# Relative attention: the order of VectorE's PSUM copy and its row maxima within a unit

## The chip, the cores and the metric

The kernel runs on one core of one Trainium2 chip. The metric is the time of one execution on the device in microseconds (us), as the median of repeated runs.

## The reference

An audio tower of five stages over x of 32 sequences x 256 frames x 7 channels: a signature tokeniser (255 tokens of 128 features for each sequence), a fuzzy attention, a top-1 mixture of 8 experts, a relative-position attention, and a top-2 mixture of 64 experts with a shared expert. Each but the first works on a layer norm of h and adds to h. The change is in the fourth, which computes this:

```python
    b, t, c = x.shape            # 32, 255, 128 here
    h, hd = (H, HD)              # 8 heads of 16
    q = x @ Wq + bq
    k = x @ Wk + bk
    v = x @ Wv + bv
    ...
    idx = _rel_index(t)          # clip(key - query, -68, 68) + 68
    rk2 = rel_k[idx]
    rv2 = rel_v[idx]
    attn1 = jnp.einsum('bhqd,bhkd->bhqk', rq, rk)
    attn2 = jnp.einsum('bhqd,qkd->bhqk', rq, rk2)
    attn = jax.nn.softmax((attn1 + attn2) * (1.0 / math.sqrt(c)), axis=-1)
    w1 = jnp.einsum('bhqk,bhkd->bhqd', attn, rv)
    w2 = jnp.einsum('bhqk,qkd->bhqd', attn, rv2)
    out = (w1 + w2).transpose(0, 2, 1, 3).reshape(b, t, c)
    return out @ Wo + bo
```

## The kernel before

The kernel is one program of stages, one behind the other. `relative_attention` is the stage of the change. Each engine has its own instruction queue, written out by hand, and works it off in order; semaphores join them. The stage takes the 32 sequences `b` one by one, each in NU = 4 units `u`; a unit is four blocks of 128 rows, a row being one query of one head. So there are 128 units, and each engine runs its `slot(b, u, r)` 128 times, between a `head` and a `tail`. The work is pipelined over units: in slot (b, u)

- TensorE first turns the exponentials of unit (b, u): `turn_e`, eight 128x128 transposes (L1748) into the one PSUM tile `t_ps`, ended by the semaphore `t_done`. Then come small products of other sequences and the content scores of the unit two ahead (`content`, L1707, three matmuls for each block), `turn_o` (L1792; in u = 0 and u = 2, it waits for this unit's `eT_v`), `positions` (L1762, from the turned exponentials with the relative values, into `rv_ps`), in odd units `values` (L1781), and last `position_scores` of the unit two ahead (L1727), which end its scores and raise `s_done`.
- ScalarE copies its half of the turned exponentials (`read_eT`, L1975), takes the exponentials of the next unit (`exps`, L1966, four instructions, with the maxima as bias, raising `e_ready`), and then has, among others, `read_n` (L1994), in u = 2 `read_q` (L1947, L1949), in every second sequence `read_odds` (L2026, u = 0), and `read_rv` (L1982), which copies `rv_ps` out and raises `rv_read`.
- VectorE takes the row maxima of the next unit (`maxima`, L2299) and copies its half of the turned exponentials (`read_eT`, L2307), and then has the work listed by unit in its `slot`: for instance the low part of the keys (`keys_remainder`, L2251, u = 2), for which TensorE's `project_q` (L1691) waits, and the choice of experts (`route`).

`turn_e` starts with these waits, so both the exponentials and ScalarE's last copy out of `t_ps` stand before it (`rv_ps` lies in `t_ps`):

```python
pe.wait_ge(e_ready, NU * b + u + 1)
if after(b, 1) or u > 0:
    pe.wait_ge(rv_read, NU * b + u)
```

There are two score tiles (`s_ps[u % 2]`) and two of exponentials (`e[u % 2]`), but one `t_ps`. GpSimd scatters rows of the next stage and SyncE moves rows through HBM beside all this.

Of the kernel before, what the change touches and what calls it, by code (L numbers as in the profile page):

```python
# [1463 lines left out]
def relative_attention(nc, K, h, mean, rstd, stats, y0_rows, o_rows, q_rows, weights, x1_slots, xT_rows, placed, y0_out, sent):  # L1464
# [3 lines left out]
    with Bench(nc, "rel") as m:  # L1468
# [93 lines left out]
        def have(b):  # L1562
            return not isinstance(b, int) or 0 <= b < B

        def after(b, n):
            return not isinstance(b, int) or b >= n
# [17 lines left out]
        def ahead(b, u, n):  # L1584
            return (b + (u + n) // NU, (u + n) % NU)
# [29 lines left out]
        with nc.Block(no_gpsimd_drain=True) as block:  # L1615
# [586 lines left out]
            def _(dve):  # L2202
                def add_rows(c):
                    hc = h[:, c * CH:(c + 1) * CH, :]
                    dve.wait_ge(y_in[c], 16)
                    nc.vector.tensor_tensor(hc, hc, y_at[c], ALU.add).then_inc(rows_added, 1)
# [58 lines left out]
                def queries_remainder(b, r, pairs):  # L2265

                    dve.wait_ge(rest_ready, b + 1)
                    if b == 0:
                        dve.wait_ge(zeroed, 4)
                    if after(b, 2):  # L2270
                        dve.wait_ge(s_done, NU * (b - 1))
                    for k in pairs:
                        nc.vector.tensor_copy(of_heads(q_head[r][1], k), of_pair(1, k).bitcast(FP32)).then_inc(ql_ready, 1)  # L2273

                def position_queries(b, r):

                    dve.wait_ge(q_in, 16 * 2 * QUAD * (b + 1))
                    if after(b, 2):
                        dve.wait_ge(s_done, NU * (b - 1))
                    nc.vector.tensor_tensor(  # L2280
                        q_pos[r][:], q_rep[:].rearrange("p h (g i) -> p g h i", i=QUAD),
                        mask4[:].unsqueeze(1).unsqueeze(1).to_broadcast([P, T // (2 * QUAD), H, QUAD]),
                        ALU.mult).then_inc(qp_ready, 1)

                def read_v(b, r):

                    dve.wait_ge(v_done, b + 1)
                    if after(b, 2):
                        dve.wait_ge(pv_done, 2 * b - 2)
                    heads = "p s (h d) -> p s h d"  # L2290
                    for k, bias_sb in ((0, bv_sb[:].unsqueeze(1).to_broadcast([P, 2, D])), (1, vends_sb[:])):
                        last = nc.vector.tensor_tensor(
                            v[r][:, :, k, :, 0:HD], pa.rearrange("p (s h d) -> p s h d", s=2, h=H),
                            bias_sb.rearrange(heads, h=H), ALU.add)
                    last.then_inc(v_ready, 1)

                def maxima(b, u):
                    dve.wait_ge(s_done, NU * b + u + 1)
                    nc.vector.tensor_reduce(neg_max[u % 2][:], s_ps[u % 2][:, :, 0:L], AX.X, ALU.max, negate=True)\  # L2299
                        .then_inc(max_ready, 1)  # L2300

                def read_eT(b, u):
                    s, n = u // 2, UB * (u % 2)
                    dve.wait_ge(t_done, NU * b + u + 1)
                    if after(b, 1):
                        dve.wait_ge(pv_done, 2 * b + s - 1)
                    nc.vector.tensor_copy(eT[s][:, 1, n:n + UB], t_ps[:, 1]).then_inc(eT_v, 1)  # L2307

                def read_ot(b, s):
                    j = 2 * b + s  # L2310
                    dve.wait_ge(ot_done, j + 1)
                    nc.vector.tensor_copy(o_tok[:], o_of[:, :, 0:HD + 1]).then_inc(ot_read, 1)

                def combine(b, s):

                    j = 2 * b + s
                    dve.wait_ge(ot_read, j + 1)
                    dve.wait_ge(rv_in, 16 * (j + 1))
                    nc.vector.reciprocal(rden[:], o_tok[:, :, HD:HD + 1].rearrange("p k c -> p (k c)"))\
                        .then_inc(rden_ready, 1)  # L2320
                    nc.vector.tensor_tensor(o_sum[:], o_tok[:, :, 0:HD],
                                            rv_tok[:, s, :].rearrange("p (h d) -> p h d", d=HD), ALU.add)\
                        .then_inc(sum_ready, 1)
                    dve.wait_ge(rden_ready, j + 1)
                    dve.wait_ge(sum_ready, j + 1)
                    if s == 1 or after(b, 1):
                        dve.wait_ge(oT_done, j)
                    nc.vector.tensor_tensor(o_norm[:], o_sum[:], rden[:].unsqueeze(2).to_broadcast([P, H, HD]),
                                            ALU.mult).then_inc(o_ready, 1)

                def add_out(b, s):
                    j = 2 * b + s
                    dve.wait_ge(out_done, j + 1)
                    hb = one_tile(h, j)
                    dve.wait_ge(bo_ready, b + 1)
                    nc.vector.tensor_tensor(hb, hb, pb[:, P:2 * P], ALU.add).then_inc(h_ready, 1)
                    dve.wait_ge(h_ready, j + 1)
                    nc.vector.bn_stats(one_tile(stats, j), hb).then_inc(stats_ready, 1)
# [101 lines left out]
                def route(bb, u):  # L2440
                    if u == 1:
                        if LAG_TOP <= bb < B + LAG_TOP:
                            best(bb - LAG_TOP)
                        if chunk_at(bb, LAG_COUNT) is not None:
                            weigh(chunk_at(bb, LAG_COUNT))
                    if u == 2:
                        if chunk_at(bb, LAG_CHOOSE) is not None:
                            choose_first(chunk_at(bb, LAG_CHOOSE))
                        if chunk_at(bb, LAG_COUNT) is not None:
                            places(chunk_at(bb, LAG_COUNT))  # L2450
                            scores(chunk_at(bb, LAG_COUNT))
                    if u == 3:
                        if chunk_at(bb, LAG_CHOOSE) is not None:
                            choose_second(chunk_at(bb, LAG_CHOOSE))
                        if chunk_at(bb, LAG_COUNT) is not None:
                            accumulate(chunk_at(bb, LAG_COUNT))

                def slot(b, u, r):
                    b1, u1 = ahead(b, u, 1)
                    if have(b1):  # L2460
                        maxima(b1, u1)
                    read_eT(b, u)
                    if u == 0:
                        if have(b + 1):
                            queries_remainder(b + 1, 1 - r, (1,))
                        if have(b - 1):
                            read_ot(b - 1, 1)
                        if have(b + 1):
                            read_v(b + 1, 1 - r)
                            queries_remainder(b + 1, 1 - r, (2, 3))  # L2470
                    if u == 1:
                        if have(b - 1):
                            add_out(b - 1, 0)
                        route(b, u)
                        if have(b - 1):
                            combine(b - 1, 1)
                        if have(b + 1):
                            position_queries(b + 1, 1 - r)
                    if u == 2:
                        if have(b + 2):  # L2480
                            keys_remainder(b + 2, r)
                        read_ot(b, 0)
                        if have(b + 3):
                            read_x(b + 3)
                    if u == 3:
                        if have(b - 1):
                            add_out(b - 1, 1)
                        combine(b, 0)
                        if have(b + 2):
                            queries_rest(b + 2)  # L2490
                            queries_remainder(b + 2, r, (0,))
                    if u >= 2:
                        route(b, u)
                    if b == 0 and u >= 1:
                        add_rows(4 + u)
                    if b == 0:
                        stats_of_rows(2 + u)
                    if b == 1 and u < 2:
                        stats_of_rows(6 + u)
# [33 lines left out]
                def tail():  # L2533
# [20 lines left out]
                    locate(nc.vector, dve, link, NC1 - 1)  # L2554

                run(slot, head, tail)


# [524 lines left out]
```

## Time and profile before

| what | value |
|---|---|
| median of 3 runs | 1923.41 us (1918.25 to 1926.46) |
| the profiled execution, whole | 1924.41 us |
| its span in the profile | 1922.3 us |
| TensorE busy | 1656.3 us, 86% |
| VectorE busy | 1402.0 us, 73% |
| ScalarE busy | 938.9 us, 49% |
| GpSimd busy | 882.1 us, 46% |

The span is what the trace covers, and 2.1 us of the execution lie around it. Busy shares are means over five stages with different limits; the 128 units of relative attention stand from about 945 to 1660 us of the span. A slot is told here from the start of its eight transposes (L1748) to the start of those of the next slot, since these are the first work of TensorE's slot.

### The profile page before, as it was taken

The numbers are of one execution on the slowest core, as the hardware profiler recorded it, in microseconds if no ns is written. First come the engines' busy times: TensorE is split into PE (matmuls) and PEld (weight loads), VectorE is DVE, ScalarE is ACT, GpSimd is POOL, SyncE is SP. The second block draws the span as 40 slices with busy tenths as digits, with TensorE's granted clock in tenths as the row PEclk, the third lists the DMA queues.
The fourth block names the chain that finished last, engine by engine and source line by source line (L and its number), as shares of the span: only waits on it lengthen the run. The fifth ranks groups of instructions, "written<-read, shape, count | busy, mean of one in ns | idle before, by whom it ended". The sixth has DMA issues, their size and how long they took to land. (4 is left out here: it accounts for less than half of the span.)

```text
span 1922.3 us, 59270 instructions
## 1 busy us (share of the span) xinstructions
PE 1656.3 (86%) x21927; PEld 1392.3 (72%) x21927; DVE 1402.0 (73%) x3369; ACT 938.9 (49%) x2305; POOL 882.1 (46%) x1710
## 2 busy tenths in 40 slices
PE   5999999999979884999599999999999999648750
PEld 4888888888858773999478888888888888525430
DVE  6777777877758884666787888888888888635434
ACT  2222212221228770677467777777777777424320
POOL 3333333333202566566232455445555555547771
PEclk9999999999989995999699999999999999869985
DMA  8900000000022001222323333333333333256537
GB/s 298 165 0 0 0 0 0 0 0 0 0 81 102 23 25 55 65 72 65 124 60 63 74 87 78 77 77 78 76 79 80 86 77 78 63 149 171 169 102 271
DMA packets 312667, 147.60 MB, mean 77 GB/s; under 512 B 205238, under 2 KB 291284, under 8 KB 312020
## 3 DMA queue, kind: packets, MB, share of 16 engines
q1 hardware_dynamic: 299876, 118.38, 25.3%
q0 software_dynamic: 12544, 25.91, 3.9%
q8 instruction: 157, 2.57, 0.6%
q14 instruction: 90, 0.74, 0.1%
HBM read 72.03 MB, written 73.37 MB: 76 GB/s over the span
## 5 line engine op out<-in xcount | busy, mean ns | idle before, releaser
L2143 POOL DMA_INDIRECT x_slots<-rel_x,rel_at x128 | 135.5, 1059 | 212.5 <-PE rel_s_ps L1727 186.9
L535 PE MATMUL tok_main_ps<-tok_w_h,tok_feat_h 128*128 128x512 f32 x512 | 205.3, 401 | 0.9 <-DVE tok_feat_low L99 0.9
L1966 ACT ACTIVATE rel_e<-rel_s_ps,rel_neg_max 128x255 f32<-128x255 f32 x512 | 200.2, 482 | 10.7 <-DVE rel_neg_max L2299 9.5
L535 PE MATMUL tok_main_ps<-tok_w_h,tok_feat_l 128*128 128x512 f32 x512 | 200.6, 392 | 0.0
L535 PE MATMUL tok_main_ps<-tok_w_l,tok_feat_h 128*128 128x512 f32 x512 | 200.3, 391 | 0.0
L2299 DVE TENSOR_REDUCE rel_neg_max<-rel_s_ps 128x4 f32<-128x1020 f32 x128 | 155.9, 1218 | 53.2 <-PE rel_s_ps L1727 51.2
L84 POOL TENSOR_TENSOR tok_q_pre<-tok_v_q,tok_v 128x128 f32 (+1 forms) x32 | 39.0, 1219 | 310.5 <-DVE tok_q L274 295.8
L1707 PE MATMUL rel_s_ps<-rel_k_h,rel_q_head_h 128*128 128x256 f32 x512 | 154.6, 302 | 0.2 <-DVE rel_q_head_l L2273 0.2
L1748 PE MATMUL rel_t_ps<-all_k_ident,rel_e 128*128 128x128 f32 x1024 | 139.3, 279 | 14.4 <-issue 14.0
L294 DVE TENSOR_TENSOR tok_prod<-tok_main_ps,tok_v 128x1024 f32<-128x1024 f32 x64 | 78.4, 1225 | 97.9 <-PE tok_main_ps L540 97.9
L1748 PEld LDWEIGHTS rel_t_ps<-all_k_ident,rel_e 128*128 128x128 f32 x1024 | 109.6, 141 | 47.0 <-issue 45.8
L1707 PE MATMUL rel_s_ps<-rel_k_l,rel_q_head_h 128*128 128x256 f32 x512 | 143.5, 280 | 0.0
L1707 PE MATMUL rel_s_ps<-rel_k_h,rel_q_head_l 128*128 128x256 f32 x512 | 143.2, 280 | 0.0
L2661 POOL DMA_INDIRECT y_rows<-exp_y,exp_x x128 | 123.4, 964 | 34.7 <-issue 33.8
L301 DVE TENSOR_REDUCE tok_inc<-tok_prod 128x128 f32<-128x1024 f32 x64 | 128.1, 2002 | 2.2
L435 ACT ACTIVATE tok_r2v_h<-tok_r2v 128x1024 fp32r<-128x1024 f32 x32 | 33.9, 1061 | 191.6 <-DVE tok_r2v L84 191.6
L1762 PE MATMUL rel_t_ps<-attn_value_table,rel_eT 128*32 128x64 f32 x6656 | 119.5, 221 | 0.8 <-DVE rel_eT L2307 0.7
L1762 PEld LDWEIGHTS rel_t_ps<-attn_value_table,rel_eT 128*32 128x32 f32 x6656 | 98.9, 110 | 24.7 <-issue 20.8
L445 ACT ACTIVATE tok_feat_h<-tok_a_ps 128x512 fp32r<-128x512 f32 x64 | 38.3, 598 | 156.8 <-PE tok_a_ps L521 136.4
L1975 ACT ACTIVATE rel_eT<-rel_t_ps 128x512 f32<-128x512 f32 x128 | 76.5, 598 | 74.9 <-PE rel_t_ps L1748 74.8
L535 PEld LDWEIGHTS tok_main_ps<-tok_w_h,tok_feat_l 128*128 128x128 f32 x512 | 96.5, 189 | 21.0
L535 PEld LDWEIGHTS tok_main_ps<-tok_w_h,tok_feat_h 128*128 128x128 f32 x512 | 97.0, 189 | 19.2 <-DVE tok_feat_low L99 1.0
(406 smaller groups left out, 4725.2 us busy)
## 6 DMA issues: line engine op xcount, KB each, us to landing
rel_q_rep<-q_rows SPq DMA_DIRECT2D x256, 64.0 KB, 2.5
o_rows<-rel_rv SPq DMA_DIRECT2D x256, 64.0 KB
x_slots<-early_zeros SPq DMA_DIRECT2D x16, 520.0 KB, 6.2
exp_x<-x_slots SPq DMA_DIRECT2D x32, 260.0 KB, 3.0
y_rows<-early_zeros SPq DMA_DIRECT2D x16, 512.0 KB, 5.8
final_y<-y_rows SPq DMA_DIRECT2D x16, 512.0 KB, 12.0
exp_x<-x_slots SPq DMA_DIRECT2D x72, 65.0 KB, 1.9
q_rows<-rel_qT SPq DMA_DIRECT2D x64, 64.0 KB
```

The source lines that it names most:

```text
L84: return nc_eng.tensor_tensor(out, left.unsqueeze(3).to_broadcast([P, n, a, c]), right.unsqueeze(2).to_broadcast([P, n, a, c]), ALU.mult)
L294: nc.vector.tensor_tensor(prod[:, s], main_ps[s][:].rearrange("p (c o) -> p c o", c=C), vt[:, bass.ds(2 * b + s, 1), :].rearrange("p n c - ...
L301: nc.vector.tensor_reduce(inc[:, s, :], prod[:, s].rearrange("p c o -> p o c"), AX.X, ALU.add).then_inc(inc_ready, 1)
L535: nc.tensor.matmul(main_ps[s][:, cols], feat[fk][:, s, j, :], w_p[wk][:, j, cols], start=(j == 0 and (fk, wk) == (0, 0)), stop=False)
L1707: nc.tensor.matmul(s_ps[u % 2][:, n, :], q_head[r][qk][:, 4 * blk:4 * blk + 4].rearrange("p c h i -> p (c h i)"), keys_for(k_p[r][kk], u), ...
L1748: last = nc.tensor.transpose(t_ps[:, t, n, :], e[u % 2][:, n, t * P:(t + 1) * P], ident[:])
L1762: last = nc.tensor.matmul(rv_ps[32 * c:32 * c + 32, n, :], eT[s][:, t, blk % (NBLK // 2), 32 * c:32 * c + 32], vtab[:, w:w + QUAD, :].rear ...
L1966: last = nc.scalar.activation(e[u % 2][:, n, 0:L], s_ps[u % 2][:, n, 0:L], ACT.Exp, bias=neg_max[u % 2][:, n:n + 1])
L1975: nc.scalar.activation(eT[s][:, 0, n:n + UB], t_ps[:, 0], ACT.Copy).then_inc(eT_a, 1)
L2143: nc.gpsimd.indirect_dma_start(x1_slots[:], bass.IndirectOffsetOnAxis(ap=at[n][:, k, t:t + 1], axis=0), x1[n][:, t, k, :], None).then_inc( ...
L2299: nc.vector.tensor_reduce(neg_max[u % 2][:], s_ps[u % 2][:, :, 0:L], AX.X, ALU.max, negate=True)\
L2661: nc.gpsimd.indirect_dma_start(y1_rows[:], bass.IndirectOffsetOnAxis(ap=x[j][:, t, ROW_AT:ROW_AT + 1].bitcast(U32), axis=0), y[j][:, t, :] ...
```

## The change

In VectorE's slot the copy of this unit's turned exponentials now comes first and the maxima of the next unit's scores second. Nothing else is changed: no instruction is added or taken away, and no wait, buffer or other queue.

```diff
                 def slot(b, u, r):
                     b1, u1 = ahead(b, u, 1)
+                    read_eT(b, u)
                     if have(b1):
                         maxima(b1, u1)
-                    read_eT(b, u)
                     if u == 0:
```

## Rows read from the trace of the kernel before

**Rows 1.** The page: the span, and busy time of each engine.

```profile
span 1922.3 us, 59270 instructions
PE 1656.3 (86%) x21927; PEld 1392.3 (72%) x21927; DVE 1402.0 (73%) x3369; ACT 938.9 (49%) x2305; POOL 882.1 (46%) x1710
```

**Rows 2.** Windows: the stage, then the slots u = 0 to 3 of b = 10.

```profile
core 0: us, PE busy (x) PEld busy (x) DVE busy (x) ACT busy (x) POOL busy (x), PEclk, DMA share, GB/s
944.00:1662.00 718.00, 681.22 (x16198) 590.01 (x16182) 594.21 (x1494) 524.62 (x1300) 347.08 (x1034) 1.00 0.34 75
...
1172.04:1176.23 4.19, 4.19 (x100) 3.63 (x96) 3.64 (x7) 3.79 (x10) 3.11 (x15) 1.00 0.55 147
1176.23:1182.37 6.14, 6.14 (x162) 5.65 (x158) 5.14 (x16) 2.71 (x7) 4.05 (x12) 1.00 0.25 47
1182.37:1188.48 6.11, 5.19 (x125) 4.26 (x122) 5.09 (x12) 5.84 (x16) 1.59 (x2) 1.00 0.36 69
1188.48:1194.14 5.66, 5.66 (x132) 4.99 (x133) 4.10 (x13) 4.24 (x10) 3.70 (x10) 1.00 0.34 74
```

**Rows 3.** Waits of TensorE in the stage: us in total, times, longest.

```profile
PE rel_t_ps L1792 <- DVE rel_eT L2307: 15.2, 22, 2.4
PE rel_t_ps L1748 <- issue: 14.0, 30, 0.9
```

**Rows 4.** Timeline of TensorE, u = 0 of b = 10: start, duration.

```profile
1172.04 1.09 PE L1748 MATMUL rel_t_ps<-all_k_ident,rel_e 128*128 128x128 f32 x8
...
1176.23 1.09 PE L1748 MATMUL rel_t_ps<-all_k_ident,rel_e 128*128 128x128 f32 x8
```

**Rows 5.** Timeline of VectorE, the same slot.

```profile
1172.18 1.22 DVE L2299 TENSOR_REDUCE rel_neg_max<-rel_s_ps 128x4 f32<-128x1020 f32 x1 [0.66 <-PE rel_s_ps L1727]
1173.31 0.68 DVE L2307 COPY rel_eT<-rel_t_ps 128x512 f32<-128x512 f32 x1
```

**Rows 6.** Timeline of ScalarE, the same slot and the start of u = 1.

```profile
1173.79 1.56 ACT L1966 ACTIVATE rel_e<-rel_s_ps,rel_neg_max 128x255 f32<-128x255 f32 x4
...
1175.60 0.38 ACT L1982 ACTIVATE rel_rv<-rel_t_ps 128x256 f32<-128x256 f32 x1
1177.36 0.60 ACT L1975 ACTIVATE rel_eT<-rel_t_ps 128x512 f32<-128x512 f32 x1 [1.38 <-PE rel_t_ps L1748]
```

**Rows 7.** Timeline of VectorE, u = 2 of b = 10.

```profile
1182.60 1.21 DVE L2299 TENSOR_REDUCE rel_neg_max<-rel_s_ps 128x4 f32<-128x1020 f32 x1
1183.73 0.68 DVE L2307 COPY rel_eT<-rel_t_ps 128x512 f32<-128x512 f32 x1
```

**Rows 8.** Timeline of ScalarE, the same slot.

```profile
1185.09 1.57 ACT L1966 ACTIVATE rel_e<-rel_s_ps,rel_neg_max 128x255 f32<-128x255 f32 x4
1186.51 0.32 ACT L1994 ACTIVATE rel_oT<-rel_pb 128x128 f32<-128x128 f32 x1
1186.67 1.07 ACT L1947 ACTIVATE rel_q_hl<-rel_pa,rel_q_bias,rel_q_scale 128x256 fp32r<-128x256 f32 x2
...
1187.92 0.46 ACT L1982 ACTIVATE rel_rv<-rel_t_ps 128x256 f32<-128x256 f32 x1
```

**Rows 9.** Timeline of TensorE, the end of the same slot.

```profile
1186.90 0.65 PE L1727 MATMUL rel_s_ps<-rel_ktab_end,rel_q_pos 64*32 64x83 f32 x32
1188.48 0.95 PE L1748 MATMUL rel_t_ps<-all_k_ident,rel_e 128*128 128x128 f32 x7 [0.93 <-issue]
```

**Rows 10.** Timeline of TensorE and VectorE, u = 2 of b = 20.

```profile
1409.67 1.09 PE L1748 MATMUL rel_t_ps<-all_k_ident,rel_e 128*128 128x128 f32 x8
...
1411.11 1.21 DVE L2299 TENSOR_REDUCE rel_neg_max<-rel_s_ps 128x4 f32<-128x1020 f32 x1
...
1412.83 0.87 DVE L2251 SCALAR_TENSOR_TENSOR rel_k_l<-rel_pa,rel_bk_end,rel_k_h 128x256 fp32r<-128x256 f32 x2
```

**Rows 11.** Waits of ScalarE, 960 to 1650 us.

```profile
ACT rel_q_hl L1947 <- PE rel_pa L1691: 2.8, 8, 0.6
```

**Rows 12.** One tile's instructions: ns min/median/max, first and last start.

```profile
L2026 ACT ACTIVATE rel_odds<-rel_top x14: 237/240/251, 1063.3 to 1647.2; 128x8 f32<-128x8 f32 x14
```

## The prediction

> **What bounds the kernel now.** I read the page first. TensorE is busy for 86% of the span, VectorE for 73%, ScalarE for less [rows 1]. That is a mean over five stages, so I went on to the windows of this stage alone. In its 718 us TensorE is busy for 681.2 us, at a granted clock of 1.00, which is the 2.4 GHz level [rows 2]. It is the bound in most places, and 37 us of idle time are all that a better order could win. Cut by unit, b = 10 shows which slots have slack: u = 0, 1 and 3 are full (4.19 busy of 4.19 us, 6.14 of 6.14, 5.66 of 5.66), u = 2 is not (5.19 of 6.11) [rows 2]. The waits say what TensorE waits for: 15.2 us, 22 times, for VectorE's copy of the exponentials before `turn_o`, and 14.0 us, 30 times, ahead of the transposes with no cause named [rows 3].
>
> The second cause can be read from u = 2 of b = 10. TensorE ends its scores at 1186.90 + 0.65 = 1187.55 and starts the next transposes at 1188.48, after 0.93 us of idleness [rows 9]. `turn_e` waits for `rv_read`, and ScalarE's `read_rv` ends at 1187.92 + 0.46 = 1188.38, 0.10 us earlier [rows 8]. So in u = 2 ScalarE's queue sets the end of the slot. In u = 0 it does not: ScalarE's `read_rv` ends at 1175.98, and TensorE, busy through the whole slot, starts the next transposes only at 1176.23 [rows 6, 4, 2].
>
> Times below count from the start of a slot's transposes.
>
> **The change in u = 0.** Before, the maxima run under the transposes: they start at 0.14 and end at 1.36, and the copy follows at 1.27 [rows 5, 4]. The exponentials start at 1.75 and end at 3.31 [rows 6]. Now nothing of VectorE's pair starts before `t_done`. ScalarE's copy, which waits for the same semaphore, shows when that is: 1177.36 - 1176.23 = 1.13, or 0.04 behind the transposes' end [rows 6, 4]. Step by step:
>
> - copy: starts 1.13, takes 0.68 [rows 5];
> - maxima: an instruction starts about 0.09 before the end shown for the one ahead (1173.31 against 1173.40) [rows 5], so 1.72, and with 1.22 they end at 2.94;
> - four exponentials: with a hand-over of 0.04, from 2.98 to 4.54 (1.56) [rows 6];
> - `read_n`: 0.15 before that end, 4.39, and what is behind it starts 0.16 later, 4.55 [rows 8];
> - `read_rv`: 0.46 [rows 8], so 5.01;
> - transposes of u = 1: 0.10 behind it [rows 8, 9], 5.11.
>
> The slot was 4.19 and full, so it grows by 0.92 us. Nothing covers this: TensorE's work of the slot is at an end at 4.19, and its next instruction needs both `e_ready` (4.54) and `rv_read` (5.01). Thirty sequences (b = 2 to 31) have this form: 30 x 0.92 = 27.6 us. The bounds: if only `e_ready` counted, (4.54 + 0.10 - 4.19) x 30 = 13.5 us; if every overlap (0.09, 0.15 and the 0.16 for a 0.32 us instruction) were missing, 0.40 more in each slot, 39.6 us. I take the middle value, since each of its steps has a row of the same queue.
>
> In 14 sequences `read_odds` (0.24 us [rows 12]) stands between `read_n` and `read_rv` in this slot. Today it is hidden by the wait for `positions`; it comes on the path now. With the overlap of small neighbours, 0.16: 14 x 0.16 = 2.2 us (bounds 0 and 3.4).
>
> **The change in u = 2.** VectorE comes late out of u = 1 here. In b = 10 the maxima start at 0.23 and the exponentials at 2.72, held by ScalarE's own queue [rows 7, 8]. With the copy at 1.13 the exponentials can't start before 2.98: 0.26 later, and as ScalarE's queue sets this slot's end, the slot grows by 0.26. Where VectorE is later than `t_done`, the order is nearly free: in b = 20 it is free at 1.44, and `keys_remainder` starts at 3.16 in either order [rows 10]; the `project_q` behind it holds ScalarE, and the exponentials end only some 0.05 later than that wait. Such slots are those in which ScalarE waits for `project_q`: 8 [rows 11]. So 22 x 0.26 + 8 x 0.05 = 6.1 us (bounds 0 and 30 x 0.26 = 7.8).
>
> Here the 15.2 us of waits for the copy [rows 3] should turn up as a gain. The copy does end earlier, by up to (1183.73 + 0.68 - 1182.37) - 1.81 = 0.23 in b = 10 [rows 7] and by some 1.1 where VectorE was late; but `turn_o` is not what ends this slot. ScalarE's queue does, or `project_q` behind `keys_remainder`, which comes after the pair in both orders. I book 0; the bound is -15.2.
>
> **u = 1 and u = 3.** The exponentials end at about 4.54 here too. In u = 1 (6.14) `read_rv` has to wait for `positions` anyway, and the slot stays full of TensorE's work. In u = 3 (5.66) a copy of 0.38 and `read_rv` follow, to about 5.3: 0.3 us of cover is left. VectorE's later work starts 0.6 to 1.1 us later; in u = 1 it then waits for the gate's logits as before, and from u = 3 it runs into the first 1.1 us of u = 0, where it would otherwise idle for `t_done`. Both at 0; if the cover in u = 1 and u = 3 were gone, some 0.26 in 62 slots, 16 us. VectorE's load, 594 of 718 us [rows 2], allows the extra idleness.
>
> The sum: 27.6 + 2.2 + 6.1 = 35.9 us. The profiled execution took 1924.4 us (span 1922.3 [rows 1] and 2.1 around it), so 1960.3; the median of runs is 1.0 below it, so 1959.
>
> A rule speaks to the overlap of 0.09. The Trainium skill, VectorE: DVE Perf Modes, section "The DRAIN you can't avoid", says that the next VectorE operation does not start until the pipe has emptied. The rows above have the copy start 0.09 before the end shown for the maxima, so the trace does not agree as its durations stand. By the rule the maxima would start at 1.81, and with 52 slots on such a path the sum would be 4.7 us more, 1964.
>
> **The rivals.**
>
> - Small loss. The longer u = 0 is partly given back, or `read_rv` is not behind the exponentials in effect, and only `e_ready` holds: +13.5, 1937. Against it: ScalarE's queue has `read_rv` behind `exps`, in order.
> - Faster. `turn_o` is the real limit in u = 2, and the earlier copy wins its 15.2 us [rows 3]: 1908. It decides if the exponentials are not needed before the end of a slot. For it: these are the largest named waits of TensorE. Against it: u = 0 is full at 4.19 and the chain through the new order can't be shorter than 1.13 + 0.68 + 1.22 + 1.56 = 4.59 less the overlaps.
> - No change: VectorE comes behind `t_done` anyway, as in b = 20 [rows 10], and the order doesn't matter: 1923. Against it: in u = 0 it waits 0.66 us for the scores and has begun the maxima at 0.14 [rows 5].
> - Spread. The cover in u = 1 and u = 3 fails as well: 1959 + 16 = 1975.
> - The clock. TensorE gets some 0.9 us more of idleness in each sequence; if the granted clock fell from 1.00 to 0.95 over the stage, 681 us of work would take 36 us more, 1995. Against it: u = 2 idles for 0.92 us in one piece, at a granted clock of 1.00 [rows 2, 9]. The Trainium skill, TensorE: Matmul & The Clock Gate, section "What's actually happening", says that the array is throttled by default and activity releases it; by that, more idleness is a risk, and the trace so far gives no sign of it.
>
> **How the numbers follow.** The forecast has 0.84, small loss 0.05, spread 0.04, clock 0.01, faster 0.03, no change 0.03. A change of under 0.5% (9.6 us) can't be told from none in this kernel. Slower is 0.84 + 0.05 + 0.04 + 0.01 = 0.94, same 0.03, faster 0.03. The forecast's own bounds are 1924 + 13.5 = 1937 and 1923 + 39.6 + 3.4 + 7.8 = 1974; since every step of the chain has a row, I give the range as 1947 to 1971, which cuts both far ends.
>
> **What would show it.** In the profile after: u = 0 slots of about 5.1 us with an idle TensorE of 0.9 us ahead of L1748, and an idle VectorE ahead of L2307 until `t_done`; u = 2 slots of about 6.37; u = 1 and 3 unchanged; the exponentials at 2.98 in nearly all slots; fewer waits of L1792 for L2307. The prediction is wrong if u = 0 stays near 4.2, if u = 2 shortens with `turn_o`, or if u = 1 and u = 3 grow.

## The result, and the profile after

The changed kernel took 1954.74 us (median; 1952.57 to 1956.59) against 1924.64 us of the kernel before (1918.25 to 1926.46): a ratio of 1.0152, 95% interval 1.013 to 1.0173, or 30.1 us. It is slower, as forecast; the forecast time was 1959 and its range 1947 to 1971.

The page's first lines, as [rows 1]:

```profile
span 1951.6 us, 59256 instructions
...
PE 1660.0 (85%) x21927; PEld 1393.1 (71%) x21927; DVE 1396.2 (72%) x3369; ACT 936.9 (48%) x2305; POOL 885.1 (45%) x1710
```

The busy time of every engine is the same within 6 us. What has grown is idleness. The windows of the stage and of the slots u = 0 to 3 of b = 10, with the columns of [rows 2], show where:

```profile
944.00:1692.00 748.00, 678.26 (x16106) 586.49 (x16106) 585.80 (x1487) 519.88 (x1294) 349.71 (x1035) 1.00 0.32 72
1178.35:1183.44 5.09, 4.26 (x99) 3.66 (x96) 4.24 (x10) 4.23 (x11) 3.70 (x18) 1.00 0.47 131
1183.44:1189.53 6.09, 6.09 (x158) 5.60 (x158) 4.95 (x15) 2.82 (x7) 3.36 (x8) 1.00 0.24 47
1189.53:1195.90 6.37, 5.27 (x126) 4.23 (x122) 4.33 (x11) 5.96 (x16) 0.97 (x1) 1.00 0.33 65
1195.90:1201.56 5.66, 5.66 (x133) 4.98 (x133) 4.34 (x12) 3.57 (x9) 3.46 (x7) 1.00 0.35 79
```

The slot u = 0 was 4.19 us and full; it is 5.09 with 4.26 busy. u = 2 went from 6.11 to 6.37, u = 1 and u = 3 stayed (6.14 and 6.09, 5.66 and 5.66). The granted clock is 1.00 in all of them. The chain in u = 0 can be followed through three timelines. VectorE:

```profile
1179.48 0.69 DVE L2307 COPY rel_eT<-rel_t_ps 128x512 f32<-128x512 f32 x1 [0.66 <-PE rel_t_ps L1748]
1180.09 1.21 DVE L2299 TENSOR_REDUCE rel_neg_max<-rel_s_ps 128x4 f32<-128x1020 f32 x1
```

ScalarE:

```profile
1181.34 1.57 ACT L1966 ACTIVATE rel_e<-rel_s_ps,rel_neg_max 128x255 f32<-128x255 f32 x4 [0.69 <-DVE rel_neg_max L2299]
1182.77 0.30 ACT L1994 ACTIVATE rel_oT<-rel_pb 128x128 f32<-128x128 f32 x1
1182.93 0.41 ACT L1982 ACTIVATE rel_rv<-rel_t_ps 128x256 f32<-128x256 f32 x1
```

TensorE:

```profile
1181.78 0.83 PE L1727 MATMUL rel_s_ps<-rel_ktab_end,rel_q_pos 64*32 64x194 f32 x32
1183.44 1.06 PE L1748 MATMUL rel_t_ps<-all_k_ident,rel_e 128*128 128x128 f32 x8 [0.83 <-ACT rel_e L1966]
```

From the slot's start at 1178.35: copy at 1.13, maxima at 1.74, exponentials at 2.99, `read_n` at 4.42, `read_rv` from 4.58 to 4.99, next transposes at 5.09. Each step of the forecast's chain is there. The profile puts the wait down to L1966; but the exponentials end at 1182.91 and `read_rv` at 1183.34, 0.10 us before the transposes start. Which one counts, the fourth experiment decides.

The waits of TensorE in the stage (944 to 1700 us), as [rows 3]:

```profile
PE rel_t_ps L1748 <- ACT rel_e L1966: 28.1, 32, 1.6
PE rel_pa L1691 <- DVE rel_k_l L2251: 26.3, 30, 1.4
PE rel_t_ps L1748 <- issue: 8.3, 30, 0.6
PE rel_t_ps L1792 <- DVE rel_eT L2307: 2.3, 2, 1.4
```

The first row is the new idleness of u = 0, 28.1 us in 32 slots. The waits for the copy fell from 15.2 to 2.3 us, and nothing came of it: a wait of 26.3 us for `keys_remainder` (L2251), which is behind the pair on VectorE, stands in their place. In u = 2 of b = 10, `keys_remainder` and TensorE's `project_q` behind it stood at 1.96 and 2.87 of the slot in the kernel before:

```profile
1184.33 0.86 DVE L2251 SCALAR_TENSOR_TENSOR rel_k_l<-rel_pa,rel_bk_end,rel_k_h 128x256 fp32r<-128x256 f32 x2
...
1185.24 0.70 PE L1691 MATMUL rel_pa<-rel_xT,attn_wq 128*128 128x256 f32 x2
```

They now stand at 2.87 and 3.79, 0.9 us later:

```profile
1192.40 0.87 DVE L2251 SCALAR_TENSOR_TENSOR rel_k_l<-rel_pa,rel_bk_end,rel_k_h 128x256 fp32r<-128x256 f32 x2
...
1193.32 0.70 PE L1691 MATMUL rel_pa<-rel_xT,attn_wq 128*128 128x256 f32 x2 [0.83 <-DVE rel_k_l L2251]
```

The transposes of the stage, first and last start, of the kernel before and of this one:

```profile
L1748 PE MATMUL rel_t_ps<-all_k_ident,rel_e x1024: 270/273/332, 947.6 to 1659.2; 128*128 128x128 f32 x171
```

```profile
L1748 PE MATMUL rel_t_ps<-all_k_ident,rel_e x1024: 269/273/331, 944.0 to 1689.4; 128*128 128x128 f32 x171
```

The stage went from 711.6 to 745.4 us: +33.8. By the starts of the transposes, the u = 0 slots hold 28.6 of it, u = 2 5.8, u = 3 0.4, and u = 1 -1.0. The span grew by 29.3 only: in this execution the stage began 3.6 us earlier and the part behind it took 0.9 us less, both in stages that the change doesn't touch.

### The profile page after: what moved, and what is told of

It is laid out like the page before. It is cut to its first block and busy times, and to the rows that moved or that the text cites. A ratio compares the mean times of both kernels' runs of the same rounds, so it can differ in the third digit from the quotient of the medians.

```text
span 1951.6 us, 59256 instructions
## 1 busy us (share of the span) xinstructions
PE 1660.0 (85%) x21927; PEld 1393.1 (71%) x21927; DVE 1396.2 (72%) x3369; ACT 936.9 (48%) x2305; POOL 885.1 (45%) x1710
## 5 line engine op out<-in xcount | busy, mean ns | idle before, releaser
L1966 ACT ACTIVATE rel_e<-rel_s_ps,rel_neg_max 128x255 f32<-128x255 f32 x512 | 200.5, 474 | 111.2 <-DVE rel_neg_max L2299 107.7
L2307 DVE COPY rel_eT<-rel_t_ps 128x512 f32<-128x512 f32 x128 | 88.4, 691 | 131.1 <-PE rel_t_ps L1748 129.6
L1748 PE MATMUL rel_t_ps<-all_k_ident,rel_e 128*128 128x128 f32 x1024 | 138.4, 278 | 38.7 <-ACT rel_e L1966 28.1
L1748 PEld LDWEIGHTS rel_t_ps<-all_k_ident,rel_e 128*128 128x128 f32 x1024 | 109.6, 141 | 72.8 <-ACT rel_e L1966 40.9
L1762 PE MATMUL rel_t_ps<-attn_value_table,rel_eT 128*32 128x64 f32 x6656 | 120.0, 221 | 0.0
L1762 PEld LDWEIGHTS rel_t_ps<-attn_value_table,rel_eT 128*32 128x32 f32 x6656 | 99.2, 110 | 23.8 <-issue 21.5
```

The costliest lines, as they stand in the source:

```text
L1748: last = nc.tensor.transpose(t_ps[:, t, n, :], e[u % 2][:, n, t * P:(t + 1) * P], ident[:])
L1762: last = nc.tensor.matmul(rv_ps[32 * c:32 * c + 32, n, :], eT[s][:, t, blk % (NBLK // 2), 32 * c:32 * c + 32], vtab[:, w:w + QUAD, :].rear ...
L1966: last = nc.scalar.activation(e[u % 2][:, n, 0:L], s_ps[u % 2][:, n, 0:L], ACT.Exp, bias=neg_max[u % 2][:, n:n + 1])
```

## The experiments

The twelve runs below were made on three chips, four on each, and each ratio is to the kernel before on the same chip: 1924.9 us on the first (`e1_u0` to `e4_rv_first`), 2001.0 on the second (`e5_halves` to `e8_after_rv2`), 1999.3 on the third (`e9_before_again` to `e12_q_later`). A figure such as +23 us is such a ratio turned into us. The slots of the first chip are compared with the trace of before; those of the second and the third with a trace of the kernel before from the third (`e9_before_again`), as there is none from the second.

One limit goes with this. The changed kernel itself ran only beside the 1924.64 us above. On the two slower chips the u = 1 slots are long in the kernel before (last section), and they are 6 to 9 us shorter in sum in each kernel in which VectorE's pair starts at the transposes' end in every slot (`e5_halves`, `e7_wait_only`, `e8_after_rv2`, `e11_after_q_later_rv2`). What the change costs on these chips is therefore not known, and where a loss measured there is set beside the 30.1 us, the slots are the better guide.

**The copy first in u = 0 only.** (`e1_u0`)

```diff
-                    read_eT(b, u)
+                    if u == 0:
+                        read_eT(b, u)
                     if have(b1):
                         maxima(b1, u1)
+                    if not (u == 0):
+                        read_eT(b, u)
```

> The copy goes first in u = 0 only; u = 1, 2 and 3 keep the order of before. Theory (the chain copy, maxima, exponentials, ScalarE's read_rv ends the slot of u = 0, and the other places pay little): u = 0 slots of 5.1 us against 4.2, some 28 us slower than before in all. Rival (the loss is spread over the units, or VectorE's waiting costs wherever it stands): about a quarter of the 30 us, 7 to 10.

Measured: 1.0119 (1.0097 to 1.0142), +23 us. The u = 0 slots are 28.4 us longer in sum, as in the full change; the u = 2 slots are 3.5 us shorter, for a reason that comes below. The rival of an even spread falls.

**The copy first in u = 2 only** (`e2_u2`: the same edit with `u == 2`).

> The copy goes first in u = 2 only. Theory: 0.26 us in most of 30 slots that ScalarE's queue ends, less where VectorE came late: 5 to 7 us slower than before. Rival (the copy's earlier end frees turn_o and wins part of the 15.2 us of waits): equal or up to 10 us faster.

Measured: 1.0044 (1.0029 to 1.0059), +8.5 us. The u = 2 slots are 6.36 us at the median, against 6.11, +7.8 in sum. Slower, so the earlier copy wins nothing there.

**The copy first in u = 1 and u = 3 only** (`e3_odd`: `u % 2 == 1`).

> The copy goes first in u = 1 and u = 3 only. Theory: both slots are full of TensorE's work and cover the later exponentials, 0 to 1 us either way, and the u = 0 slots stay at 4.2. Rival (spread): 10 us or more slower than before.

Measured: 1.0035 (1.0021 to 1.0048), +6.7 us. Neither expectation holds. u = 1 and u = 3 themselves changed by 0.2 and 0.1 us in sum, as the theory has it; but the u = 0 slots, whose order is that of before, are 4.43 at the median in place of 4.19, +8.2 us in sum. The timeline of b = 10, u = 0 (start at 1169.64):

```profile
1169.10 1.93 ACT L1958 ACTIVATE rel_q_head_h<-rel_q_hl 32x512 fp32r<-32x512 f32 x3
...
1171.34 0.60 ACT L1975 ACTIVATE rel_eT<-rel_t_ps 128x512 f32<-128x512 f32 x1
1171.96 1.57 ACT L1966 ACTIVATE rel_e<-rel_s_ps,rel_neg_max 128x255 f32<-128x255 f32 x4
...
1173.56 0.41 ACT L1982 ACTIVATE rel_rv<-rel_t_ps 128x256 f32<-128x256 f32 x1
1174.07 0.30 PE L1748 MATMUL rel_t_ps<-all_k_ident,rel_e 128*128 128x128 f32 x1
```

The later exponentials of u = 3 push the end of ScalarE's rounding of the queries (L1958) to 1.39 us into u = 0 (0.81 before: 1170.92 + 1.93, with a start at 1172.04). Its copy then starts at 1.70 (1.13 before), the exponentials at 2.32 (1.75 before), and `read_rv` ends at 4.33, 0.10 before the transposes. So u = 3 has a bill of some 8 us, presented in u = 0. (That it is u = 3 and not u = 1 rests on this timeline; the two weren't run apart.) In the full change it doesn't show, because the chain there holds the exponentials until 2.98 anyway. The growths of the stage in the three kernels, 25.7, 9.6 and 10.4 us, add up to 45.7; together they cost 33.8.

**The changed kernel, with `read_rv` of u = 0 ahead of `read_n` and `read_odds`.** (`e4_rv_first`)

```diff
+                    if u == 0:
+                        read_rv(b, u)
                     if u == 0 and have(b - 1):
                         read_n(b - 1, 0)
...
-                    if u % 2 == 0:
+                    if u == 2:
                         read_rv(b, u)
```

> The changed kernel, and in u = 0 ScalarE's read_rv stands directly behind the exponentials, ahead of read_n and read_odds. Theory (rv_read is the last of the two waits of the next transposes): each u = 0 slot 0.16 us shorter, another 0.10 in 14 of them: 5 to 7 us less than the changed kernel, some 24 us slower than before. Rival (e_ready is the last, as the profile after names it): nothing, 30 us slower than before.

Measured: 1.0127 (1.0107 to 1.0148), +24.4 us. The stage is 739.3 us, 6.1 less than with the change alone, and the u = 0 slots are 4.92 at the median. In b = 10 (start at 1175.54):

```profile
1178.52 1.57 ACT L1966 ACTIVATE rel_e<-rel_s_ps,rel_neg_max 128x255 f32<-128x255 f32 x4 [0.69 <-DVE rel_neg_max L2301]
1179.96 0.40 ACT L1982 ACTIVATE rel_rv<-rel_t_ps 128x256 f32<-128x256 f32 x1
1180.23 0.30 ACT L1994 ACTIVATE rel_oT<-rel_pb 128x128 f32<-128x128 f32 x1
1180.46 0.41 PE L1748 MATMUL rel_t_ps<-all_k_ident,rel_e 128*128 128x128 f32 x2 [0.66 <-ACT rel_e L1966]
```

The exponentials stand where they stood (2.98), and the transposes moved with `read_rv`, 0.10 behind it. So `rv_read` is the last wait, though the profile still names L1966. The rival in which only `e_ready` counts falls.

**The changed kernel, with the maxima in two halves.** (`e5_halves`)

```diff
-                    nc.vector.tensor_reduce(neg_max[u % 2][:], s_ps[u % 2][:, :, 0:L], AX.X, ALU.max, negate=True)\
-                        .then_inc(max_ready, 1)
+                    for k in range(2):
+                        n = slice(UB // 2 * k, UB // 2 * k + UB // 2)
+                        nc.vector.tensor_reduce(neg_max[u % 2][:, n], s_ps[u % 2][:, n, 0:L], AX.X, ALU.max, negate=True)\
+                            .then_inc(max_ready, 1)
...
                     for n in range(UB):
+                        if n % (UB // 2) == 0:
+                            act.wait_ge(max_ready, 2 * (NU * b + u) + 1 + n // (UB // 2))
```

> The changed kernel with the maxima as two instructions of two blocks each, so that the exponentials of a unit start when the first half is done. Theory (the chain from the transposes' end through copy, maxima and exponentials sets u = 0 and u = 2): the chain is shorter by half of the maxima, some 0.55 us: u = 0 slots of 4.55, u = 2 slots back at 6.1; 16 + 6 = 22 us less than the changed kernel, 8 us slower than before. Rival (VectorE's load or its waiting costs, not the chain): equal or slower than the changed kernel, since VectorE has one instruction more per unit.

Measured: 1.0049 (1.0036 to 1.0062), +9.8 us, about a third of the 30.1 us that the change cost on the other chip; by the slots, u = 0 has 12.7 us of its 28.6 left and u = 2 all of its growth (+6.8). The u = 0 slots are 4.62 (4.72 with `read_odds`), as the chain predicts. The u = 2 slots are not back at 6.1; they are 6.35. b = 10, u = 2 (start at 1205.06):

```profile
1206.79 1.27 DVE L2302 TENSOR_REDUCE rel_neg_max<-rel_s_ps 128x2 f32<-128x510 f32 x2
...
1207.78 1.58 ACT L1967 ACTIVATE rel_e<-rel_s_ps,rel_neg_max 128x255 f32<-128x255 f32 x4
1207.98 0.86 DVE L2252 SCALAR_TENSOR_TENSOR rel_k_l<-rel_pa,rel_bk_end,rel_k_h 128x256 fp32r<-128x256 f32 x2
...
1208.90 0.70 PE L1691 MATMUL rel_pa<-rel_xT,attn_wq 128*128 128x256 f32 x2 [0.89 <-DVE rel_k_l L2252]
...
1209.64 1.02 ACT L1947 ACTIVATE rel_q_hl<-rel_pa,rel_q_bias,rel_q_scale 128x256 fp32r<-128x256 f32 x2
```

The exponentials start at 2.72, as before the change. But `keys_remainder` is still behind the pair, `project_q` waits 0.89 us for it, and ScalarE's `read_q` for that. In u = 2 of the new order there is thus a second chain, of the same length within 0.02 us.

**The kernel before, with `read_rv` of u = 2 ahead of `read_q`.** (`e6_before_rv2`)

```diff
-                    if u % 2 == 1:
+                    if u > 0:
                         read_rv(b, u)
...
-                    if u % 2 == 0:
+                    if u == 0:
                         read_rv(b, u)
```

> The kernel before, with ScalarE's read_rv of u = 2 ahead of read_q. Theory (in u = 2 the end of read_rv on ScalarE's queue sets the slot, 0.93 us after TensorE's scores): the slot falls from 6.10 to some 5.3, as read_rv then ends 0.4 us after positions: 20 to 25 us faster than before. Rival (the unnamed gap ahead of the transposes is issue time of TensorE's own queue): no change; or the later read_q comes back as a wait of its own in u = 3 and takes most of it.

Measured: 1.0008 (0.9991 to 1.0025), no difference. The u = 2 slots are 6.06 at the median. In b = 10 (start at 1202.30):

```profile
1201.70 0.20 DVE L2319 RECIPROCAL rel_rden<-rel_o_tok 128x8 f32<-128x8 f32 x1 [2.42 <-DMA rel_rv_tok<-o_rows]
...
1202.36 1.22 DVE L2280 TENSOR_TENSOR rel_q_pos<-rel_q_rep,all_k_mask 128x1024 f32<-128x1024 f32 x1
...
1205.22 0.86 DVE L2251 SCALAR_TENSOR_TENSOR rel_k_l<-rel_pa,rel_bk_end,rel_k_h 128x256 fp32r<-128x256 f32 x2
...
1206.14 0.70 PE L1691 MATMUL rel_pa<-rel_xT,attn_wq 128*128 128x256 f32 x2 [0.17 <-DVE rel_k_l L2251]
...
1207.94 0.38 ACT L1982 ACTIVATE rel_rv<-rel_t_ps 128x256 f32<-128x256 f32 x1 [1.18 <-PE rel_t_ps L1762]
```

ScalarE now waits 1.18 us for `positions`, so its queue no longer sets the slot; `project_q`, waiting for `keys_remainder`, does. But `keys_remainder` starts at 2.92 here and at 1.96 in the kernel before. VectorE came late into the slot, after a wait of 2.42 us in u = 1 for rows that SyncE turns through HBM; in the stage (960 to 1720 us) such waits are

```profile
DVE rel_rden L2319 <- DMA rel_rv_tok<-o_rows: 27.1, 22, 2.8
```

against 8.2 us, 10 times, in `e9_before_again`. Where VectorE is not late, the theory holds: in eight slots of b = 2 to 29 (seven of them with even b), u = 2 lasts 5.13 to 5.29 us. The others lie at 5.57 and above, up to 9.28 (b = 5), and the u = 2 slots are 4.7 us shorter in sum. So the second limit is `project_q` behind a VectorE that comes late, and the expectation of 20 us overlooked it. The trace is of an execution of 1993.77 us, and the twelve took 1993.3 to 2010.4, so its slots may be shorter than most.

**The order of before, but the maxima wait for the transposes as well.** (`e7_wait_only`)

```diff
                     if have(b1):
+                        dve.wait_ge(t_done, NU * b + u + 1)
                         maxima(b1, u1)
                     read_eT(b, u)
```

> The order of before (maxima, then copy), but the maxima wait for the transposes' end as well, so that VectorE starts its pair as late as in the changed kernel and only the order differs. Theory: in u = 0 the exponentials start at 1.13 + 1.22 + 0.04 = 2.4 and the slot ends at 4.5 by ScalarE's queue; the copy ends at 2.95 against 2.47 of the content scores, which delays turn_o and what is behind it by some 0.5: slots of 4.7, some 15 us slower than before; in u = 2 the exponentials stay at 2.72. So the waiting alone is half of the loss and the copy ahead of the maxima the other half. Rival (the wait is all that costs, and the order nothing): 28 to 30 us slower.

Measured: 1.0141 (1.0114 to 1.0168), +28.2 us, the loss that the rival's number gave. In sum the slots u = 0, 2 and 3 are 24.4, 5.2 and 4.5 us longer and u = 1 8.7 shorter; in the changed kernel they were 28.6, 5.8 and 0.4 longer and 1.0 shorter. The u = 0 slots are 5.00 (the theory said 4.7; it let `turn_o` be delayed from 2.47, but it stood at 2.31 in the kernel before). b = 10, u = 0 (start at 1201.41):

```profile
1202.54 1.22 DVE L2299 TENSOR_REDUCE rel_neg_max<-rel_s_ps 128x4 f32<-128x1020 f32 x1 [0.74 <-PE rel_t_ps L1748]
1203.68 0.68 DVE L2307 COPY rel_eT<-rel_t_ps 128x512 f32<-128x512 f32 x1
...
1204.51 0.41 PE L1792 MATMUL rel_t_ps<-all_k_ident,rel_oS 128*128 128x128 f32 x2 [0.53 <-DVE rel_eT L2307]
```

Here the slot is set by the other user: `turn_o` waits for the copy, 3.10 into the slot, and positions and scores follow it. So once VectorE starts its pair only at the transposes' end, the order within the pair matters little (34.1 against 34.8 us in the three kinds of slot); either the exponentials are late or the copy is. What the order of before is worth is the 1.1 us in which the maxima run under the transposes.

**The changed kernel, with `read_rv` of u = 2 ahead of `read_q`** (`e8_after_rv2`: the edit of `e6_before_rv2`).

> The changed kernel, with read_rv of u = 2 ahead of read_q. Theory: u = 2 slots of some 5.3 to 5.6 in place of 6.37, the u = 0 slots stay at 5.1: 20 to 28 us less than the changed kernel, about the time of before. Rival (no slack behind ScalarE's queue): as the changed kernel.

Measured: 1.0113 (1.0097 to 1.013), +22.6 us; by the ratios 8 us less than the change, not 20 to 28, and part of that may be the chip's. The u = 2 slots are 6.07 (6.37 in the changed kernel), where the second limit holds them: `project_q` starts at 3.79, as in the changed kernel. u = 0 stays at 5.09.

**The kernel before again, with its profile.** (`e9_before_again`)

> The kernel before, unchanged, for its slots on the chip of the runs beside it: no difference, and u = 0 and u = 2 slots of 4.2 and 6.1 us.

Measured: 1.0008 (0.9996 to 1.002). u = 0 and u = 2 slots have the medians 4.21 and 6.11, as on the first chip; the stage is 731.5 us long instead of 711.6, and the u = 1 slots are 19.5 us longer.

**Both limits of u = 2 lifted, on the kernel before** (`e10_q_later_rv2`). The edit of `e6_before_rv2`, and on TensorE:

```diff
                             turn_n(b - 1, 1)
-                        if have(b + 2):
-                            project_q(b + 2)
...
                     positions(b, u)
+                    if u == 2 and have(b + 2):
+                        project_q(b + 2)
```

> The kernel before, with two edits in u = 2: read_rv ahead of read_q on ScalarE, and project_q behind positions on TensorE. Theory (u = 2 has two limits close together: read_rv at the end of ScalarE's queue, and project_q behind VectorE's keys_remainder, with positions and the scores queued behind it; only both edits together free the slot): u = 2 slots of 5.3 in place of 6.1, some 22 us faster than before. Rival (the later read_q returns as a wait in u = 3 or u = 0, or the two limits are not all): within 5 us of before.

Measured: 0.996 (0.9946 to 0.9974), 8 us faster than before, and the fastest of all kernels here against the kernel before beside it. Far less came of it than the 22 us expected. With b = 24, u = 2 lasts 5.13 us (1520.31 to 1525.44), as the theory has it, and it is under 5.35 in ten slots of b = 2 to 29. It is longer in most with odd b, up to 9.57 (b = 7, from 1127.22) and 9.20 (b = 27, from 1587.11). The waits of VectorE and of TensorE (960 to 1720 and 960 to 1700 us) point to the cause:

```profile
DVE rel_rden L2319 <- DMA rel_rv_tok<-o_rows: 28.8, 24, 2.5
```

```profile
PE rel_t_ps L1792 <- DVE rel_eT L2307: 24.1, 21, 3.1
```

VectorE's `combine` in u = 1 needs the rows from HBM, as in `e6_before_rv2`, and the shorter slots leave less time for their trip. VectorE comes late into u = 2, and with it the copy for which `turn_o` waits. That this wait is what took the rest was read from the trace; no run changed the trip.

**The same two edits on the changed kernel.** (`e11_after_q_later_rv2`)

> The changed kernel with the same two edits. Theory: u = 0 slots stay at 5.1, u = 2 slots fall from 6.37 to some 5.4, 25 us less than the changed kernel and about the time of before. Rival (the new order's chain ends u = 2 as well): exponentials to 4.55 and read_rv to 5.1 leave the slot at 5.2 at least, so no rival below that; if read_q pushes ScalarE's u = 3 and u = 0, half of the gain is lost.

Measured: 0.999 (0.9975 to 1.0005), the time of before. The u = 0 slots are 5.09 (5.19 with `read_odds`), the u = 2 slots 5.14 at the median. In sum the u = 2 slots are 24.8 us shorter than those of before, where the same edits on the order of before made them 6.7 shorter; the longer u = 0 (+28.5) uses that up, and only the u = 1 slots (-7.4) leave the stage 3 us shorter. The order of before stays ahead by 0.3% (4 us at the median). VectorE's waits for the rows are 16.8 us (17 times) here, against 28.8, and what is left of its lateness is mostly covered, since its pair in u = 2 can't start before 1.13 in any case: `keys_remainder` starts at 2.86 to 2.88 in most slots.

**`project_q` behind positions alone, on the kernel before.** (`e12_q_later`)

> The kernel before, with project_q behind positions alone; read_rv stays behind read_q. Theory: read_q now waits for the later project_q and holds read_rv behind it, so u = 2 slots grow to some 7: 20 to 30 us slower than before. Rival (read_rv's place is of no weight): faster, as with both edits.

Measured: 1.0036 (1.0022 to 1.005), +7 us. The direction is the theory's, the size is not: `positions` no longer waits for `project_q` and runs from 3.07 to 4.17 at the median, `project_q` follows it at once, and `read_rv` behind `read_q` ends at 6.50, so the slot is 6.63 and not 7. The u = 2 slots are 16.7 us longer in sum, u = 1 and u = 3 4.1 and 2.5 shorter; what shortened these is open.

## Why the prediction was right

- What bounds the slots. Right: u = 0, 1 and 3 full, u = 2 ended by ScalarE's queue with 0.93 us of idleness. Lifting that limit alone gained nothing in time (`e6_before_rv2`): `project_q` behind `keys_remainder` took over wherever VectorE came late. The prediction named this second limit for the late slots only.
- u = 0. Forecast a slot of 5.11 and 27.6 us, and 2.2 more for `read_odds`; measured 5.09 without and 5.19 with `read_odds` (0.10, not 0.16), 28.6 us in all, of which 28.0 in b = 2 to 31. The sum took 0.46 for `read_rv` from u = 2, where the row of u = 0 itself had 0.38; measured 0.41. The exponentials and `read_n` started 0.01 and 0.03 later than forecast, so the step errors nearly cancel, which is a small piece of luck. That `read_rv` and not the exponentials is the last step is shown by `e4_rv_first`; that the chain runs through the maxima, by `e5_halves` (4.62).
- The overlap. The maxima start at 1180.09, the copy ends at 1179.48 + 0.69 = 1180.17: an overlap of 0.08, where the step had 0.09. The Trainium skill, VectorE: DVE Perf Modes, section "The DRAIN you can't avoid", says that the next operation does not start until the pipe has emptied; the sum that the prediction worked out from this (1964) was not borne out. The prediction left out that the same paragraph goes on "A next op that is not held starts earlier", so the overlap does not contradict the section. Whether this pair counts as held no run here shows.
- u = 2. Forecast 22 x 0.26 + 8 x 0.05 = 6.1 us for b = 2 to 31; measured 5.8 in all, but 4.6 in these and 1.3 in b = 0 and 1, which the sum didn't have. The 0.26 of the ordinary slots is right; that the sums agree so closely is luck. Even the 0.26 has two causes: `e5_halves` put the exponentials back to 2.72, and the slot stayed at 6.35, held by `keys_remainder`, which the prediction had as a limit in the late slots only. The 8 late slots were taken over from the trace of before, and they did not stay: nearly every u = 2 slot is now 6.36 to 6.37, also b = 9, which was 6.56. VectorE's waits for the rows from HBM (960 to 1720 us), before and after:

```profile
DVE rel_rden L2319 <- DMA rel_rv_tok<-o_rows: 7.0, 10, 1.3
```

```profile
DVE rel_rden L2319 <- DMA rel_rv_tok<-o_rows: 1.6, 2, 0.8
```

  With 0.9 us more in u = 0, the rows are there in time and VectorE is not late. The same goes for `e1_u0`, where these waits are 0.6 us (2 times) and the u = 2 slots 3.5 us shorter.
- The 15.2 us of waits for the copy. Booked at 0, and right: they fell to 2.3, and `e2_u2` was slower.
- u = 1 and u = 3. Booked at 0; measured -1.0 and 0.4. But `e3_odd` shows that the cover of u = 3 was not what the step said: it counted ScalarE's queue up to `read_rv` and left out the rounding of the queries behind it (L1958, 1.93 us). That work spills into u = 0 and costs 8 us there unless something larger stands in front of it.
- The sum. Forecast +35.9 against a stage longer by 33.8 and a median longer by 30.1 (by the interval, 25 to 33). The stage's sum was 2 us high: 1.2 in u = 0 (0.8 of it `read_odds`), 0.3 in u = 2, and 1.0 by which u = 1 shortened, less 0.4 in u = 3. The other 4 us lie outside the stage. In the trace of before it starts at 947.6 us, in those of the changed kernel and of `e1_u0` to `e4_rv_first` at 942.8 to 944.0; what makes this is open.
- The rivals. Faster and no change fell with the result. Small loss was 1937 and fell with `e4_rv_first`. Spread had 1975: u = 1 and u = 3 did not grow in sum. The granted clock of the stage stayed at 1.00.

## What to carry to other kernels

In an in-order queue, put first the instruction whose input is there first, and price a swap as a chain through every engine to the first instruction that waits for its end, not as the sum of waits it removes: 15.2 us of named waits were worth nothing here, and 1.1 us of cover under the transposes was worth 28. Ask of each slot what the second limit is before taking away the first, and don't add up the costs of parts tested alone: 45.7 us of them made 33.8. Where the profile names one of two semaphores as the releaser, look for an instruction that ends just before the start.

## What the hardware showed that was not expected

The kernel before took 2001.0 us on the second chip and 1999.3 on the third, 4% more than the 1924.9 of the first. Between the traces of the first and the third, the spans differ by 76 us: 14 ahead of the stage, 20 in it and 42 behind it. The transposes of L1748 take 273 ns at the median on both. Behind the stage TensorE's granted clock falls from 1.00 to 0.50 again and again on the third chip, with a mean of 0.74 there against 0.79 on the first, where it held 1.00 from 1714 to 1861 us; the matmuls of L2714 take 778 ns at the mean against 645. But in the trace of the changed kernel the clock also fell again and again in that part, and it took no longer (262.2 us against 263.1), so the clock alone does not explain the 42 us. In the stage the difference is in the u = 1 slots, which are 6.5 us on the first chip at most sequences with odd b and 6.1 with even b, but 7.6 or 7.7 on the third with many even b from 8 on. In such a slot TensorE stands still before or within L1762 with no releaser, as in `e8_after_rv2`:

```profile
1207.74 0.55 PE L1762 MATMUL rel_t_ps<-attn_value_table,rel_eT 128*32 128x64 f32 x22 [0.44 <-issue]
```

In b = 8, 10, 22, 24 and 28 `e9_before_again` has two such stops in the slot; `e8_after_rv2` and `e11_after_q_later_rv2`, with the changed order, have one (b = 10, 22 and 28), and the slot is 7.0 to 7.1 us. What holds the queue there was not tried.

The other surprise is the trip of the rows through HBM: with shorter slots VectorE's waits for it went from 8.2 us (10 times, `e9_before_again`) to 28.8 us (24 times, `e10_q_later_rv2`), and little of what the edits won in single slots was left in the time.
